# Two gather stages of a graph-network kernel: TensorE's sums signal once for two groups, and other products are seen with the next sums

## The reference

```python
xn = _layernorm(x, axis=-1)
x = x + _L0_gnn_ref(xn, edge_index, ...) + _L0_mix_ref(xn[None], ...)[0]
x = x + _L0_ffn_ref(_layernorm(x, axis=-1)[None], ...)[0]
xn = _layernorm(x, axis=-1)
x = x + _L1_gnn_ref(xn, edge_attr_4, edge_attr_10, ..., src, dst) + _L1_mix_ref(xn[None], ...)[0]
x = x + _L1_ffn_ref(_layernorm(x, axis=-1)[None], ...)[0]
```

## Time and profile before

| | us |
|---|---|
| runs, median (lowest, highest of 3) | 3297.3 (3295.75, 3297.57) |
| profiled execution: its time | 3321.8 |
| profiled execution: its span, first to last instruction | 3320.2 |
| PE busy | 2798.5 (84%) |
| PEld busy | 2306.8 (69%) |
| DVE busy | 1720.7 (52%) |
| ACT busy | 1425.6 (43%) |
| POOL busy | 1775.9 (53%) |
| mean granted TensorE clock | 0.918 |

### The profile page before, as it was taken

The page is one execution under the profiler, slowest core; times in us unless marked ns, Lnnn a source line. Parts: engine busy times, 40 slices in busy tenths (PEclk is TensorE's granted clock), DMA queues, the critical chain, the costliest instruction groups (busy, mean ns, idle before and its releaser), DMA issues. The chain is left out here.

```text
span 3320.2 us, 52314 instructions
## 1 busy us (share of the span) xinstructions
PE 2798.5 (84%) x14715; PEld 2306.8 (69%) x14715; DVE 1720.7 (52%) x5294; ACT 1425.6 (43%) x3977; POOL 1775.9 (53%) x1889
## 2 busy tenths in 40 slices
PE   1888898899888899799957888888887777779998
PEld 1667777777777788588845555555676666668887
DVE  5742223577665566545544545555555555653333
ACT  4012222244222455255556766676645654532221
POOL 5666666666666155456666666666666566610000
PEclk9999998999998999799978988988888888889999
DMA  7244344666665376345553433433345544442222
GB/s 218 78 118 122 115 125 124 200 200 204 204 204 182 120 237 212 110 142 164 167 156 100 116 108 104 116 107 111 105 136 147 148 138 129 136 124 75 74 74 63
DMA packets 270570, 457.96 MB, mean 138 GB/s; under 512 B 75154, under 2 KB 194685, under 8 KB 269206
## 3 DMA queue, kind: packets, MB, share of 16 engines
q1 hardware_dynamic: 190642, 238.08, 24.1%
q0 software_dynamic: 78912, 215.69, 22.5%
q10 hardware_dynamic: 750, 1.08, 0.1%
HBM read 342.87 MB, written 111.83 MB: 137 GB/s over the span
## 5 line engine op out<-in xcount | busy, mean ns | idle before, releaser
L2616 POOL DMA_INDIRECT g_got<-xm_d,idx x782 | 768.4, 983 | 458.6 <-issue 212.4
L916 POOL DMA_INDIRECT g_got<-xn_d,idx x654 | 655.6, 1002 | 374.7 <-issue 186.9
L2228 PEld LDWEIGHTS ps<-g_hotw,g_got 128*128 128x128 f32 x3128 | 441.6, 209 | 207.7 <-issue 206.5
L2228 PE MATMUL ps<-g_hotw,g_got 128*128 128x128 f32 (+11 forms) x3128 | 469.1, 298 | 132.3 <-issue 67.1
L1300 PEld LDWEIGHTS ps<-g_hot,g_got 128*128 128x128 f32 x2616 | 351.3, 205 | 82.2 <-issue 74.1
L1300 PE MATMUL ps<-g_hot,g_got 128*128 128x120 f32 (+4 forms) x2616 | 362.5, 288 | 46.4 <-issue 35.2
L2671 ACT ACTIVATE g_hotw<-g_hot,g_wr 128x16 f32<-128x16 f32 (+8 forms) x1308 | 299.3, 312 | 49.2 <-DVE g_hot L627 30.8
L2761 DVE TENSOR_TENSOR g_ring<-g_ring,ps 128x84 f32 (+10 forms) x391 | 133.0, 340 | 346.5 <-DMA jobs_d<-gin_hid 158.9
L1481 POOL TENSOR_TENSOR p_ln_rs<-p_ln_pre,neg_half 125x2 f32<-125x2 f32 x50 | 35.1, 703 | 454.5 <-DVE p_ln_pre L1476 454.5
L2901 PE MATMUL ps<-g_half 128*125 128x512 f32 x400 | 228.0, 721 | 44.9 <-ACT g_half L2645 17.1
L1107 DVE TENSOR_TENSOR g_ring<-g_ring,ps 128x40 f32 (+8 forms) x327 | 68.7, 210 | 329.6 <-remote 200.4
(11 more groups left out here) (391 smaller groups left out, 5135.9 us busy)
## 6 DMA issues: line engine op xcount, KB each, us to landing
h_d<-gin_hid SPq DMA_DIRECT2D x23, 1000.0 KB
gin_hid<-h_d SPq DMA_DIRECT2D x23, 1000.0 KB
job_in<-jobs_d SPq DMA_DIRECT2D x54, 258.0 KB
g_got<-xm_d,idx POOLq DMA_INDIRECT x782
p_z<-z_d SPq DMA_DIRECT2D x49, 224.0 KB
g_got<-xn_d,idx POOLq DMA_INDIRECT x654
q_d<-g_qo SPq DMA_DIRECT2D x25, 250.0 KB
g_wqkv<-q_d SPq DMA_DIRECT2D x25, 250.0 KB
```

The costliest lines, as they stand in the source:

```text
L916: landed.start(e.indirect_dma_start(got[:, k % (2 * GB), :], None, xn_d[0:N, :], bass.IndirectOffsetOnAxis(ap=idx[:, HT + k:HT + k + 1], a ...
L2228: mm = e.matmul(to, rows[j][:, c * P:(c + 1) * P], hotw[:, j, c * w:4 * w].unsqueeze(1).broadcast_to([P, r, n]), start=(j == 0), stop=(j = ...
L2616: landed.start(e.indirect_dma_start(got[:, 2 * (g % GB) + j, :], None, xm_d[0:N, :], bass.IndirectOffsetOnAxis(ap=idx[:, 2 * g + j:2 * g + ...
```

## The change

A class `Shown` takes the place of `Steps` for the semaphores of TensorE's other products. Such a product signals only if its step is later than the last `sums` (`alone`). Otherwise its last instruction adds to nothing, and its reader waits on `summed` for the first signal of `sums` at the same step or a later one. `sums` signals only behind every second group, so its waits count pairs: group n is seen with signal n // 2. For that, `sums` is moved from the first plan of TensorE's `timeline` to the last, so that it is the last work of its step. A step with a signal comes every 4 steps in `g1` (13, 17, 21, ...) and every 2 in the second stage (6, 8, 10, ...). `square` waits once for both projections. Nothing that is computed changes, nor the steps of any stage, nor the rings. The signals of `count`, `denominators`, `product` of `g1`, `turn_radial` of `g1`, `mix_*` stay.

```diff
+class Shown:
+    def __init__(self, sem, when, lag, summed, sums_at):
+        self.sem, self.summed, self.sums_at = sem, summed, sums_at
+        self.steps = [s + lag for s in when]
+
+    def alone(self, i):
+        return self.steps[i] > self.sums_at[-1]
+
+    def done(self, ins, i):
+        if self.alone(i):
+            ins.then_inc(self.sem, 1)
+
+    def wait(self, eng, i):
+        if i >= 0 and self.alone(i):
+            eng.wait_ge(self.sem, sum(self.alone(k) for k in range(i + 1)))
+        elif i >= 0:
+            self.summed.wait(eng, sum(at < self.steps[i] for at in self.sums_at), "sums")
@@ g1
+            SUMS = [s + LEAD for s in GROUPS[1::2]] + ([GROUPS[-1] + LEAD] if NGL % 2 else [])
+            def shown(name, when, lag):
+                return Shown(ph.sem(name), when, lag, summed, SUMS)
+            heavy, xturn, kvs = shown("heavy", QKV, 7), shown("xturn", QKV, 8), shown("kvs", QKV, 25)
+            proj = {"kv0": shown("kv0", QKV, 14), "kv1": shown("kv1", QKV, 15), "q": shown("q", QKV, 16)}
+            hturn, up = shown("hturn", UPS, 0), [shown(f"up{q}", UPQ[q], 0) for q in range(4)]
+            rturn, eturn, hidden = shown("rturn", WTS, 2), shown("eturn", EDGE, 1), shown("hidden", EDGE, 5)
@@ gather
-                            summed.wait(e, k // 2 - GB, "sums")
+                            summed.wait(e, (k // 2 - GB) // 2, "sums")
@@ accumulate
-                        summed.wait(e, min(n | 1, NGL - 1), "sums")
+                        summed.wait(e, n // 2, "sums")
@@ sums
-                        summed.done(mm, "sums")
+                        if g % 2 or g == NGL - 1:
+                            summed.done(mm, "sums")
@@ turn_x, and so for each of the products above
-                        xturn.done(mm, "T")
+                        xturn.done(mm, i)
@@ copy_emb
-                        eturn.wait(e, i, "turn")
-                        hidden.wait(e, i - 2, "hid")
+                        eturn.wait(e, i)
+                        hidden.wait(e, i - 2)
@@ TensorE's timeline
                     timeline(LAST_STEP,
-                             (GROUPS, [(sums, LEAD)]),
                              (COUNT, [(count, 1)]),
...
-                             ([EDGE[-1]], [(turn_radial, 12)]))
+                             ([EDGE[-1]], [(turn_radial, 12)]), (GROUPS, [(sums, LEAD)]))
@@ second_gather
+            eturn, hidden, rturn = shown("eturn", RAD, 1), shown("hidden", RAD, 5), shown("rturn", CHUNKS, 11)
+            kturn, proj, dots = shown("kturn", KV, 2), shown("proj", KV, 5), shown("dots", KV, 14)
+            rows, turn = shown("rows", P9, 4), shown("turn", F3, 3)
@@ square
+                        proj.wait(e, i)
                         for q, bank, to, name, copy in ((0, KB, k1, "k", "raw"), (H1, V, v1, "v", "copy")):
-                            proj.wait(e, i, name)
@@ accumulate
-                        summed.wait(e, last_of(g), "sums")
+                        summed.wait(e, g // 2, "sums")
```

More of the change, by code:

```diff
@@ L735, in gps_kernel @@
             tallied = ph.steps("tallied", "add0", "add")
-            heavy = ph.steps("heavy", "sums")
             joined = ph.steps("joined", "add")
@@ L840, in load_xn @@
                         xrs.wait(e, i - 2, "t1")
-                        heavy.wait(e, i - 2, "sums")
+                        heavy.wait(e, i - 2)
                         xn_in.start_rows(e, xn[:, i % 2, :, :], spread(xn_d[0:N, :])[:, 2 * i:2 * i + 2, :], i % 2)
@@ L937, in stage @@
                             acts.done(e.activation(rk[:, t, :], ps[0:TN, 6 + t, 0:D], ACT.Relu), f"rk{t}")
-                            kvs.wait(e, i - 1, "kv")
+                            kvs.wait(e, i - 1)
                             acts.done(e.activation(v1[:, t, :, 0:P], ps[0:TN, 6 + t, D:2 * D].rearrange("p (c n) -> p c n", c=DC),
@@ L1023, in blank_rows @@
                     def blank_rows(i):
-                        heavy.wait(e, NB - 1, "sums")
+                        heavy.wait(e, NB - 1)
                         e.memset(attr4[96:RR, :, :], 0.0).then_inc(s_z, 1)
@@ L1078, in join_heavy @@
                     def join_heavy(i):
-                        heavy.wait(e, i, "sums")
+                        heavy.wait(e, i)
                         joined.wait(e, i - 1, "add")
@@ L1087, in make_hot @@
                         g, w = n + HP, WINS[n + HP]
-                        summed.wait(e, n - HR, "sums")
+                        summed.wait(e, (n - HR) // 2, "sums")
                         ready.done(one_hot(e, hot[:, n % HR, :, 0:w], rel[:, g, :], w), "hot")
@@ L1140, in acc_kv @@
                     def acc_kv(i):
-                        kvs.wait(e, i, "kv")
+                        kvs.wait(e, i)
                         accd.wait(e, i - 1, "acc")
@@ L1284, in sum_heavy @@
                                               counts_of(2 * i + t), start=(t == 0), stop=(t == 1))
-                        heavy.done(mm, "sums")
+                        heavy.done(mm, i)
                     def sums(g):
@@ L2486, in second_gather @@
             kn = ph.steps("kn", "k")
-            dots = ph.steps("dots", "dots")
             s_b = ph.sem("b")
             x_in = ph.landing("xi", XI, 2)
-            rows = ph.steps("rows", "rows")
             biased = ph.steps("biased", "xb")
@@ L2516, in second_gather, with shown @@
             LAST_STEP = P9[-1] + 28
+            SUMS = [s + LEAD for s in GROUPS[1::2]] + ([GROUPS[-1] + LEAD] if NG % 2 else [])
+            def shown(name, when, lag):
+                return Shown(ph.sem(name), when, lag, summed, SUMS)
+            eturn, hidden, rturn = shown("eturn", RAD, 1), shown("hidden", RAD, 5), shown("rturn", CHUNKS, 11)
+            kturn, proj, dots = shown("kturn", KV, 2), shown("proj", KV, 5), shown("dots", KV, 14)
+            rows, turn = shown("rows", P9, 4), shown("turn", F3, 3)
             SPARE = next(i for i in range(NT) if F3[i] + 3 > RAD[-1] + 24)
@@ L2612, in gather @@
                     def gather(g):
-                        summed.wait(e, g - GB, "sums")
+                        summed.wait(e, (g - GB) // 2, "sums")
                         e.sem_inc(s_held["Pool"], 1)
@@ L2630, in zero @@
                     def zero(b):
-                        rows.wait(e, b - RB, "rows")
+                        rows.wait(e, b - RB)
                         to = ring[:, :, cols(b)]
@@ L2667, in weigh @@
                         scaled.wait(e, n - 1, "wr")
-                        summed.wait(e, g - HR, "sums")
+                        summed.wait(e, (g - HR) // 2, "sums")
                         w = WINS[g]
@@ L2826, in x3_of @@
                         r = i % XR
-                        rows.wait(e, i, "rows")
+                        rows.wait(e, i)
                         biased.wait(e, i, "xb")
@@ L2862, in sums @@
                         added.wait(e, BEFORE[g], "add")
-                        summed.done(edge_sums(e, bank_of(g)[0], [got[:, 2 * (g % GB) + j, :] for j in range(2)],
-                                              hotw[:, g % HR, :, :], WINS[g], bank_of(g)[1]), "sums")
+                        mm = edge_sums(e, bank_of(g)[0], [got[:, 2 * (g % GB) + j, :] for j in range(2)],
+                                       hotw[:, g % HR, :, :], WINS[g], bank_of(g)[1])
+                        if g % 2 or g == NG - 1:
+                            summed.done(mm, "sums")
                     def turn_emb(i):
@@ L2897, in project @@
                         kcopy.wait(e, i, "T")
-                        for bank, name, at in ((KB, "k", 0), (V, "v", INNER)):
-                            squares.wait(e, i - 1, "raw" if name == "k" else "copy")
+                        for bank, copy, at in ((KB, "raw", 0), (V, "copy", INNER)):
+                            squares.wait(e, i - 1, copy)
                             for c in range(DC):
@@ L2952, in turned @@
                                              ident[0:TN, 0:TN])
-                        turn.done(mm, "turn")
-                    timeline(LAST_STEP, (GROUPS, [(sums, LEAD)]), (RAD, [(hidden_of, 5), (turn_emb, 1)]), (CHUNKS, [(turn_radial, 11)]),
+                        turn.done(mm, i)
+                    timeline(LAST_STEP, (RAD, [(hidden_of, 5), (turn_emb, 1)]), (CHUNKS, [(turn_radial, 11)]),
                              (KV, [(products, 14), (project, 5), (turn_k, 2)]), (MIX, [(mix_wo, 1), (mix_wq, 3)]), (F3, [(turned, 3)]),
-                             (P9, [(product, 4)]))
+                             (P9, [(product, 4)]), (GROUPS, [(sums, LEAD)]))
         with g2:
```

98 lines of the change are left out of this document (42 added, 56 removed).

## The result

| | before | changed |
|---|---|---|
| median (lowest, highest of 4), us | 3297.4 (3295.8, 3301.3) | 3399.0 (3389.6, 3407.2) |
| ratio, 95% interval | | 1.0305 [1.0289, 1.0321] |
| span of the profiled execution, us | 3320.2 | 3396.4 |
| POOL's first to last gather, first stage | 1013.0 | 1043.4 |
| from there to the second stage's first gather | 632.8 | 631.8 |

A forecast was written before the change was run, and what follows sets the result against it. It took late, queued TensorE signals, worsened by back-to-back gathers, to bound both gather stages. Terms -157 - 53 + 36 + 19 = -155 us took 3297.3 to about 3140 us; range 2990 to 3310, forecast case 3070 to 3210.

The forecast's parts named there:

- What bounds the stages: Both gather stages: POOL waits for late signals of sums, 187.7 us in the first and 246.1 us in the second.
- stages without gathers don't move: Sign to check: stages that don't gather should keep their time; if they move, the reading is wrong.
- The gain on TensorE: Gather stages: fewer queued signals remove three quarters of TensorE's 210 us of stalls, -157 us, bounds 0 and -260.
- second rival: Gather stages: one late signal suffices, a queue of instructions fills, fewer signals help little; 3240 to 3290 us, chance 0.25.
- The clock: Gather stages: a quarter of TensorE's lost clock speed comes back, -53 us, between 0 and half.
- The chain at 398 + 4j: `turn_emb` to `hidden_of`: no slack, TensorE waits for ACT's silu and copy in 16 units, +36 us, bounds +22 and +85.
- The later sight elsewhere: Second stage, `turned`, `product` and `x3_of`: readers see products up to a step later, +19 us, bounds 0 and +150.
- The gathers' wait for a pair: Ring of gathered rows: a gather waits for a whole pair, one group less every other time; costed at nothing.
- The third: Rival: readers' waits take over at 398 + 4j, `turned` and `product`, stalls little changed; about 3350 us, chance 0.16.
- The fourth: Rival: delay has nothing to do with the number of signals and the chains are covered; 3297 us, chance 0.04.
- The first: Rival: TensorE's stalls all go, half the clock returns, chains cost their lower bounds; -345, some 2960 us, chance 0.13.
- delays that grow with the distance of signals: Stated failure condition: signal delays growing with the distance between signals, since every wait in the stages hangs on sums.

The follow-up runs named there:

- k1: Kernel before, but a gather waits for the second group of the pair that used its ring place; signals late: 3370.9 against 3327.7 us, 1.0117.
- j1: Kernel before, but a gather waits for the second group of the pair that used its ring place; signals prompt: 2916.6 us, 0.9995.
- i1: Changed kernel with 1106 removed signals issued again to semaphores nobody waits for; signals late: 3409.0 against 3321.8 us for the kernel before, 1.0269.
- f0: Kernel before, unchanged, run beside the changed one for its trace; signals late: 3316.6 us.
- f1: Changed kernel, unchanged, run beside the kernel before; signals late: 3408.7 us, 1.0273.
- e4: Kernel before with only sums moved last in TensorE's step; signals prompt: 2920.6 us, 1.0007.
- i4: Kernel before with only sums moved last in TensorE's step; signals late: 3334.6 us, 1.0037.
- i3: Changed kernel's late sight of products, but sums signal every group and ring users wait as before; signals late: 3375.2 us, 1.0150.
- k2: Same kernel as i3, in another session with late signals: 3372.3 us, 1.0144.
- i2: Kernel before, but sums signal every second group and ring users wait for the pair; signals late: 3358.9 us, 1.0126.
- f3: Kernel before with six already met waits ahead of each gather; signals late: 3372.5 us, 1.0167.
- j2: Kernel before with one group less in each ring of gathered rows; signals prompt: 2918.8 us, 1.0005.
- e3: Changed kernel, but sums signal for every group, so 797 signals fewer than the kernel before; signals prompt: 2921.8 us, 1.0008.
- j4: Kernel before with two small chained memsets on POOL ahead of each gather; signals prompt: 3106.2 us, 1.0639.

## Why the prediction was wrong, point by point

- **What bounds the stages: right.** POOL waits for the signals of sums, and these are late. k1 and j1 are the proof from both sides: moving that wait by at most one group costs 1.2% when signals are late and nothing when they are prompt. That stages without gathers don't move held, too.
- **The gain on TensorE, -157 us: wrong, the main error.** I took it that the stall needs several signals in the queue. i1 holds the waits fixed and puts 1106 signals back: nothing changes, neither the time nor the idle time by "issue". The control that I had left unweighed was in the same timeline, where the crawl began behind a single late signal; that was my second rival. The trace lets one count how far TensorE gets. These rows stand between the last two of the earlier trace rows:

```profile
315.16 0.74 PE L1283 MATMUL ps<-gin_hid,g_xn 125*128 125x188 f32 x3 [0.40 <-issue]
316.59 0.32 PE L1283 MATMUL ps<-gin_hid,g_xn 125*128 125x188 f32 x1 [0.70 <-issue]
317.31 0.43 PE L1313 MATMUL ps<-ident,g_xr 125*128 125x125 f32 x2 [0.40 <-issue]
318.72 0.27 PE L1313 MATMUL ps<-ident,g_xr 125*128 125x125 f32 x1 [0.98 <-issue]
319.45 0.30 PE L1313 MATMUL ps<-ident,g_xr 125*128 125x125 f32 x1 [0.47 <-issue]
```

  Behind the outer products 24 + 3 + 1 + 2 + 1 = 31 matmuls start; their addition is recorded at 319.41, and the next matmul starts at 319.45. It is so everywhere: of all signals that can be matched in the twelve late traces (1449 in the kernel before, 1380 in i1), some were undelivered while 31 matmuls started behind them, with weight loads 62 instructions, and none while 32 did. One late signal is enough, and the bound is the same with many signals (f0, i1) and with few (f1): it goes by instructions, not by signals. Why TensorE slows after 24 already stays open. Less "issue" is no gain by itself: the time by which its rows fell is time in which TensorE now waits by name for ACT or DVE, and f1 and i1 show it alike. The Trainium skill's figure (page "TensorE: Matmul & The Clock Gate", section "The cost: per-tile semaphore tail", about 26 ns for each increment in the tail behind a run of tiles) isn't seen as a price of each signal here: i1 leaves room for at most some 11 ns.
- **The clock, -53 us: wrong.** It stayed at 0.94 and 0.86. The term stood on stalls that would go, and they didn't. In e4, where signals are prompt and the same work takes 850 and 1008 us, the granted clock is 0.99 and 0.94.
- **The chain at 398 + 4j, +36 us: over-sized.** It is there, but TensorE's wait for the copy before `hidden_of` grew from 7.2 to 16.7 us only, weight loads and matmuls counted together (line L1403, now L1424); in the rows of the matmuls alone it is 3.3 and 7.4 us:

```profile
  ACT g_embT L1021: 16.7, 17
```

- **The later sight elsewhere, +19 us: under-sized, and in the wrong place.** I priced one row, `turned`, which went from 18.7 to 24.9 us. `hidden_of` and `project` of the second stage, which I took to have slack, hold 101 us more, the latter by the order (i4). Both halves of the later sight together (i3, k2) cost 1.44 to 1.50%, 48 to 50 us at 3320, with the order's 12 in it (i4). I had 55 for the readers and nothing for the order: about the right sum by luck, from the wrong rows. The slack in steps was real, but a step is no time for ACT and DVE when they stand in queues of their own and wait for the same late event.
- **The gathers' wait for a pair, "at nothing": wrong.** It is 1.17 to 1.26%, about 40 us (k1, i2). I wrote that POOL waits for delayed signals and not for room. But the room is what decides how late a signal may be before POOL stands still: k1 takes away at most one group of it and nothing else, and POOL's waits in the first stage go from 188 to 216 us. The signal of the second group comes a step later, and the delay comes on top.
- **The rivals.** The third, slower by the readers' waits, was right in sign and kind; its 3350 us lacked the gathers' wait. 3350 and 40 give 3390, for 3399 measured, with the luck just named in the 3350. The second was right in what it said of TensorE, and POOL's pauses fell from 239 to 190, a fifth; but each grew from 1.8 to 2.5 us, where it had held them fixed. The fourth was right that the number of signals doesn't matter and wrong that the readers were covered. The first fell with i1.
- **What would make it wrong.** I named delays that grow with the distance of signals. They shrank, from a mean of 2.5 and 2.9 us to 1.5 and 1.4 (of the sums' signals alone from 2.3 and 2.7 to 1.6 and 1.4), and it got slower all the same: what counts is when the event comes on which the next work depends, not how late a signal is on average.

Not settled: why signals are late in some sessions, and whether gathers back to back have a part in it. By themselves they aren't enough, against the prediction's reading: in e4 89% of the gathers start at most 1.35 us after the one before, against 76% in the kernel before, and no signal comes more than 1.1 us late. In late sessions the two do go together: of the signals other than the sums' that came over 2 us late in the kernel before, 310 of 404 came while POOL stood still for more than its usual 0.3 us, which is about a sixth of the time. But POOL's pauses end with a signal themselves, so this doesn't tell cause from effect. Not settled either: what the six waits of f3 cost. No kernel here was clearly faster than before.

## What to carry to other kernels

Before signals are merged to save them, put them back in a copy where nobody waits for them: if the time doesn't move, only the waits count, and a merged signal can only make these later. A signal that several engines wait for turns each delay into an idle time of all of them, and slack counted in steps of a hand-written order is no slack on an engine whose earlier instruction waits for the same event. A wait for room in a ring was free here while its event was prompt (j1, j2) and cost 1.2% where it was late (k1): room is worth counting in the delay of the event that gives it back. And a wait in a profile row isn't its price: rows can grow by 67 us where the time grows by 12 (i4).

## What the runs showed of the hardware

- The same kernel takes 2918 or 3320 us on the same chip, by whether TensorE's signals come after 0.35 us or after 2.5 to 2.9 us in the stretches with gathers; each of these five sessions had one or the other throughout. A ratio is worth something only within one, and whether a small edit costs anything can hang on it: j1 is 0.9995 and k1, the same kernel, 1.0117.
- 1106 additional signals in the two gather stages cost nothing that can be measured where signals are late (i1), and 797 fewer bring nothing where they are prompt (e3).
- TensorE started at most 31 matmuls, with weight loads 62 instructions, behind one whose signal wasn't delivered yet. This bound is reached and not passed in each of the twelve late traces.
- In late sessions a part of the semaphore additions is missing from the record: of 1471 that DVE alone issued in the first gather stage of the kernel before, 938 are recorded; in the prompt session none of 1488 is missing (e4). So "remote" as a releaser in such a trace can be an ordinary signal that wasn't recorded.
- Six waits that are already met, ahead of an indirect transfer, don't lengthen the distance to the next one (1.26 us with and without, f3); two memsets of 128x4 do, to 1.38 (j4).
